# Small and wide matmul rounds grouped, and the 16 small tiles of a round taken image by image

## What is computed

```python
x = x + _L0_conv_ref(_gn(x), w3, b3, w5, b5, wr, br)   # a 3x3 and a 5x5 convolution, 9 shifts of the
                                                       # first, mixed by wr: one 5x5 filter with a border ring
x = x + _L1_conv_ref(_gn(x), filters)                  # all products of two values of the 10 (a one and
                                                       # the 3x3 patch), weighted by a 32x32x10x10 filter
```

## Time and profile before

| | |
|---|---|
| median of 3 runs | 304.58 us (304.39 to 304.66) |
| the profiled execution: own time | 305.6 us |
| its span, first to last instruction | 303.9 us |
| TensorE busy | 276.0 us (91%), 6464 matmul records |
| VectorE busy | 251.5 us (83%) |
| ScalarE busy | 88.1 us (29%) |
| mean granted TensorE clock | 0.979 |

### The profile page before, as it was taken

One profiled execution on the slowest core, in us unless ns is written; L12 is line 12 of the kernel. 1 busy time (PEld: TensorE's weight loads), 2 busy tenths in 40 slices (PEclk: granted clock), 3 DMA queues, 4 the chain that ended last, 5 costly groups with the idle time before them and its releaser, 6 DMA issues.

```text
span 303.9 us, 13566 instructions
## 1 busy us (share of the span) xinstructions
PE 276.0 (91%) x6464; PEld 125.6 (41%) x6464; DVE 251.5 (83%) x216; ACT 88.1 (29%) x135; POOL 33.0 (11%) x82
## 2 busy tenths in 40 slices
PE   0579999899999999999999999999999999999930
PEld 0124443343334434436457455333334446447310
DVE  1899899995999999599999999976999999950330
ACT  5432016949258989529000000004000000000000
POOL 7913970000110000000000000000000000000000
PEclk9999999979999999999999999999999999999985
DMA  6973000000000000000000000085000000000049
GB/s 191 382 193 82 4 3 2 2 5 2 2 2 4 4 2 2 4 2 5 2 2 4 4 2 4 2 172 111 2 2 4 2 2 4 2 4 4 2 86 190
DMA packets 19206, 11.45 MB, mean 38 GB/s; under 512 B 17744, under 2 KB 17872, under 8 KB 19024
## 3 DMA queue, kind: packets, MB, share of 16 engines
q1 hardware_dynamic: 14640, 9.06, 11.7%
q10 hardware_dynamic: 4512, 1.53, 2.2%
HBM read 6.40 MB, written 4.19 MB: 35 GB/s over the span
## 4 chain that ended last, share of the span: by engine, by line
PE 80%; DVE 7%; ACT 3%; issue 3%; DMA 2%; SPq 1%; DVEq 0%
PE acc L1007 63%; PE acc L1050 15%; ACT raw L507 3%; DMA raw<-in_x 2%; DVE stats L741 2%; PE acc L1101 2%; DVE plane L759 1%; DVE raw L801 1%; DVE arena L669 1%; ACT arena L497 1%; DVE scaled L637 0%; DVE norm L756 0%; SPq L314 0%; SPq L321 0%; DVE mean_var L746 0%
## 5 line engine op out<-in xcount | busy, mean ns | idle before, releaser
L1007 PE MATMUL acc<-product,weight 32*32 32x512 f32 (+1 forms) x3040 | 128.6, 605 | 0.0
L1007 PEld LDWEIGHTS acc<-product,weight 32*32 32x32 f32 (+1 forms) x3040 | 61.7, 110 | 63.8 <-issue 51.1
L879 DVE TENSOR_TENSOR product<-plane 128x4096 f32<-128x4096 f32 x19 | 83.3, 4427 | 0.1
L1007 PE MATMUL acc<-raw,weight 32*32 32x512 f32 (+1 forms) x992 | 44.3, 605 | 0.0
L1050 PE MATMUL acc<-product,middle 32*64 32x512 f32 (+1 forms) x576 | 30.6, 621 | 0.0
L1007 PEld LDWEIGHTS acc<-raw,weight 32*32 32x32 f32 (+1 forms) x992 | 20.4, 111 | 20.7 <-issue 16.2
L801 DVE TENSOR_TENSOR raw<-acc,arena 128x512 f32<-128x512 f32 x16 | 9.9, 684 | 18.9 <-issue 18.7
L741 DVE BATCH_NORM_STATS2 stats<-raw 128x6 f32<-128x512 f32 x32 | 19.7, 686 | 3.1 <-DMA raw<-in_x 3.1
L879 DVE TENSOR_TENSOR raw<-plane 128x4096 f32<-128x4096 f32 x5 | 22.2, 4433 | 0.0
L1007 PE MATMUL acc<-product,arena 32*32 32x512 f32 (+1 forms) x448 | 22.0, 606 | 0.0
L507 ACT ACTIVATE raw<-arena 32x512 f32<-32x512 f32 x32 | 21.9, 683 | 0.5
(11 more groups left out here) (121 smaller groups left out, 213.9 us busy)
## 6 DMA issues: line engine op xcount, KB each, us to landing
raw<-in_x SPq DMA_DIRECT2D x8, 512.0 KB, 8.5
out<-raw SPq DMA_DIRECT2D x24, 128.0 KB, 2.9
arena<-in_L_conv_filters SPq DMA_DIRECT2D x4, 400.0 KB, 6.9
out<-raw ACTq DMA_DIRECT2D x8, 128.0 KB, 4.6
arena<-in_L_conv_w ACTq DMA_DIRECT2D x4, 100.0 KB, 4.0
w_in<-in_L_conv_w ACTq DMA_DIRECT2D x2, 36.0 KB, 1.9
w_in<-in_L_conv_w SPq DMA_DIRECT2D x2, 36.0 KB, 2.1
b_in<-in_L_conv_b SPq DMA_DIRECT2D x2, 0.5 KB
```

The lines of the kernel that those rows point to most:

```text
L879: nc.vector.tensor_tensor(both_halves(g, u), plane_halves(g), plane_halves(g, PRODUCTS[k][0] * PITCH + PRODUCTS[k][1]), ALU.mult)\
L1007: return nc.tensor.matmul(acc[32 * s:32 * (s + strips), j, r, :], weights[32 * r:32 * r + 32, t:t + strips, :] .rearrange("p t c -> p (t c ...
```

## The change

Four edits, all to what TensorE issues and in what order; every matmul of before is still there, with the same operands, apart from start and stop flags that follow the order.

1. In `column`, a small round loops over images outside and strips inside (`column0`, the same form in stage 1, keeps its order).
2. The units of stage 2 that were issued as wide, small or small, wide one by one are issued in groups: several units wide, then the same units small.
3. Around the borders of group 1 in stage 1, two rounds of the wide form of "total" stand between the row edges and the column edges, where its small round stood, and the parts after them begin with the small form; in stage 2 the plane's small rounds stand ahead of the row edges, and its wide rounds between the two sets of edges.
4. Products (1,-2) and (2,-1) change places, for VectorE, GpSimd and TensorE alike.

```diff
-PRODUCTS = ((0, 0), (0, 1), (1, 1), (1, -1), (0, 2), (2, 2), (2, -2), (2, 1), (1, 2), (2, -1), (1, -2), (2, 0), (1, 0))
+PRODUCTS = ((0, 0), (0, 1), (1, 1), (1, -1), (0, 2), (2, 2), (2, -2), (2, 1), (1, 2), (1, -2), (2, -1), (2, 0), (1, 0))
 N_PRODUCTS = len(PRODUCTS)
...
-                    for s in range(STRIPS):
-                        for r in range(GROUP):
+                    for r in range(GROUP):
+                        for s in range(STRIPS):
                             d, t = (lo, 0) if s % 2 else (hi + 1, hi - lo)
                             last = tile(r, s, 1, d, t, start, stop)
                 return last
@@ -1041,7 +1041,7 @@
...
             product0(1, "next", 0, True, False, True)
             product0(1, "next", 0, False, False, False)
             edges0(0, ROW_SIDES)
-            product0(1, "total", 0, False, False, False)
+            product0(1, "total", 0, False, False, True, (-1, 0))
             edges0(0, COLUMN_SIDES)
-            product0(1, "total", 0, False, True, True).then_inc(part_done, 1)
+            product0(1, "total", 0, False, False, True, (1, 2))
+            product0(1, "total", 0, False, True, False).then_inc(part_done, 1)
             pe.wait_ge(edges_copied, 2)
-            rest0(1, PAIRS_FIRST)
+            rest0(1, SINGLES_FIRST)
...
                 if g == 0:
                     pe.wait_ge(even_ready, NG)
                     for half in (0, 1):
-                        column(0, plane_pixels(0, half), every_row, sum_taps[0][:, 0:3, :], half == 0, False, PAIRS)
+                        column(0, plane_pixels(0, half), every_row, sum_taps[0][:, 0:3, :], half == 0, False, SINGLES)
                     edges0(1, ROW_SIDES)
                     for half in (0, 1):
-                        column(0, plane_pixels(0, half), every_row, sum_taps[0][:, 0:3, :], False, False, SINGLES)
+                        column(0, plane_pixels(0, half), every_row, sum_taps[0][:, 0:3, :], False, False, PAIRS)
                     edges0(1, COLUMN_SIDES)
                     pe.wait_ge(borders, 5)
-                    mixed_unit(g, 0, "square", SP, stop=True).then_inc(shared_done, 1)
+                    mixed_unit(g, 0, "square", SINGLES)
+                    mixed_unit(g, 0, "square", PAIRS, stop=True).then_inc(shared_done, 1)
                     pe.wait_ge(edges_copied, 2 * NG)
+                    mixed_unit(g, 1, "linear", PAIRS, start=True)
+                    mixed_unit(g, 1, "square", PAIRS)
+                    mixed_unit(g, 1, "linear", SINGLES).then_inc(unit_used, 1)
+                    mixed_unit(g, 1, "square", SINGLES, stop=True).then_inc(unit_used, 1)
+                    pe.wait_ge(shared_kept, 1)
+                    side_unit(g, 0, "linear", SINGLES, start=True)
+                    side_unit(g, 0, "square", SINGLES)
+                    wait_made(g, NEXT)
+                    taps1(g, 0, NEXT, SINGLES)
+                    side_unit(g, 0, "linear", PAIRS)
+                    side_unit(g, 0, "square", PAIRS)
+                    taps1(g, 0, NEXT, PAIRS)
+                    pe.wait_ge(shared_kept, 2)
+                    side_unit(g, 1, "linear", PAIRS, start=True)
+                    side_unit(g, 1, "square", PAIRS)
+                    taps1(g, 1, NEXT, PAIRS)
+                    side_unit(g, 1, "linear", SINGLES).then_inc(unit_used, 1)
+                    side_unit(g, 1, "square", SINGLES).then_inc(unit_used, 1)
+                    taps1(g, 1, NEXT, SINGLES).then_inc(unit_used, 1)
+                    in_pairs = False
                 else:
                     pe.wait_ge(borders, 6)
                     pe.wait_ge(evicted, GROUP)
-                    mixed_unit(g, 0, "linear", PS, start=True)
-                    mixed_unit(g, 0, "square", SP)
+                    mixed_unit(g, 0, "linear", PAIRS, start=True)
+                    mixed_unit(g, 0, "square", PAIRS)
                     pe.wait_ge(stream_made, made(g, "next"))
                     column(0, stream_pixels(g, NEXT, 0), every_row, next_sum, False, False, PAIRS)
+                    mixed_unit(g, 0, "linear", SINGLES)
+                    mixed_unit(g, 0, "square", SINGLES)
                     column(0, stream_pixels(g, NEXT, 0), every_row, next_sum, False, True, SINGLES)\
                         .then_inc(shared_done, 1)
                     pe.wait_ge(evicted, 2 * GROUP)
-                mixed_unit(g, 1, "linear", SP if g else PS, start=True).then_inc(unit_used, 1)
-                mixed_unit(g, 1, "square", PS if g else SP, stop=True).then_inc(unit_used, 1)
...
-                in_pairs = g == 0
+                    mixed_unit(g, 1, "linear", SINGLES, start=True)
+                    mixed_unit(g, 1, "square", SINGLES)
+                    mixed_unit(g, 1, "linear", PAIRS).then_inc(unit_used, 1)
+                    mixed_unit(g, 1, "square", PAIRS, stop=True).then_inc(unit_used, 1)
+                    pe.wait_ge(shared_kept, 3)
+                    side_unit(g, 0, "linear", PAIRS, start=True)
+                    side_unit(g, 0, "square", PAIRS)
+                    side_unit(g, 0, "linear", SINGLES)
+                    side_unit(g, 0, "square", SINGLES)
+                    side_unit(g, 0, "next", SINGLES)
+                    side_unit(g, 0, "next", PAIRS)
+                    pe.wait_ge(shared_kept, 4)
+                    side_unit(g, 1, "linear", PAIRS, start=True)
+                    side_unit(g, 1, "square", PAIRS)
+                    side_unit(g, 1, "next", PAIRS)
+                    side_unit(g, 1, "linear", SINGLES).then_inc(unit_used, 1)
+                    side_unit(g, 1, "square", SINGLES).then_inc(unit_used, 1)
+                    side_unit(g, 1, "next", SINGLES).then_inc(unit_used, 1)
+                    in_pairs = False
```

More of the change, by code:

```diff
@@ L1042, in plane_pixels, with column0 @@
                 return pixels
-            def column0(odd, stack, at, pitch, x0, every, five, start, stop, pairs):
+            def column0(odd, stack, at, pitch, x0, every, five, start, stop, pairs, rows):
                 def tile(r, s, strips, d, t, first_one, last_one):
@@ L1054, in column0 @@
                 if pairs:
-                    for d in range(-1, 3):
+                    for d in rows:
                         for s in (0, 2):
@@ L1064, in column0, with product0 @@
                 return last
-            def product0(g, name, odd, start, stop, pairs):
+            def product0(g, name, odd, start, stop, pairs, rows=range(-1, 3)):
                 if name == "next":
@@ L1070, in product0 @@
                     return column0(odd, plane[g], PLANE_AT - 2 * PITCH, PITCH, 2, 2, weight0[:, PAIR_AT:EDGE_AT, :],
-                                   start, stop, pairs)
+                                   start, stop, pairs, rows)
                 source, x0 = ("step", 1) if name == "step after" else (name, 0)
@@ L1077, in product0 @@
                 pe.wait_ge(middle_ready, g + 1)
-                return column0(odd, *half_at(g, source), x0, 1, five, start, stop, pairs)
+                return column0(odd, *half_at(g, source), x0, 1, five, start, stop, pairs, rows)
             def part(g, names, odd, forms):
@@ L1169, in mixed_unit, with side_unit @@
                     taps = (cross_taps if j else sum_taps)[0][:, 3:6, :]
-                for pairs in forms:
-                    last = column(j, stream_pixels(g, UNIT_OF[name][0], j), every_row, taps,
-                                  start and pairs == forms[0], stop and pairs == forms[-1], pairs)
-                return last
-            def side_unit(g, j, name, forms, start=False):
+                return column(j, stream_pixels(g, UNIT_OF[name][0], j), every_row, taps, start, stop, pairs)
+            def side_unit(g, j, name, pairs, start=False):
                 pe.wait_ge(stream_made, made(g, name + (" right" if j else " left")))
@@ L1181, in side_unit @@
                     a = {"linear": 0, "square": 9}[name] + 6 * j
-                for pairs in forms:
-                    last = column(j, stream_pixels(g, UNIT_OF[name][1], j), every_row, weight1[:, a:a + 3, :],
-                                  start and pairs == forms[0], False, pairs)
-                return last
+                return column(j, stream_pixels(g, UNIT_OF[name][1], j), every_row, weight1[:, a:a + 3, :],
+                              start, False, pairs)
             def taps1(g, j, u, pairs, stop=False):
@@ L1227, in _ @@
                     pe.wait_ge(evicted, 2 * GROUP)
-                mixed_unit(g, 1, "linear", SP if g else PS, start=True).then_inc(unit_used, 1)
-                mixed_unit(g, 1, "square", PS if g else SP, stop=True).then_inc(unit_used, 1)
-                pe.wait_ge(shared_kept, 2 * g + 1)
-                side_unit(g, 0, "linear", SP if g else PS, start=True)
-                side_unit(g, 0, "square", PS if g else SP)
-                if g:
-                    side_unit(g, 0, "next", SP)
-                else:
-                    wait_made(g, NEXT)
```

(13 more changed lines are left out.)

3 lines of the change are left out of this document (1 added, 2 removed).

## The result

| | before | after |
|---|---|---|
| median | 304.66 us, 7 runs (304.39 to 305.73) | 302.79 us, 7 runs (301.44 to 304.24) |
| the profiled execution: own time, span | 305.6, 303.9 us | 304.24, 302.5 us |
| mean granted TensorE clock in it | 0.979 | 0.984 |

The ratio is 0.9925, with a 95% interval from 0.9899 to 0.9952: 0.75% faster. The forecast was 300.6 us, 2.2 too low. All ratios leave out one execution of the kernel before, 406.97 us at a mean granted clock of 0.663.

A forecast was written before the change was run, and what follows sets the result against it. TensorE, busy 91% of the span and holding 80% of the last-ending chain, was taken as the bound. 303.9 - 2.5 - 1.5 = 299.9 us of span, 301.6 own time, median 1.0 lower: 300.6 us; 8-in-10 range 297.2 to 304.6.

The forecast's parts named there:

- Term 1: Borders of stage 1: shorter instruction gap and a clock that stays high start stage 2 at 89.2, gain 2.2 us.
- rival B: Small rounds: image order makes them dearer, 0.10 us per round, 114 rounds, +11.9 us, 312.5 us; chance 0.18.
- C: Small rounds after unit 16: image order makes them cheaper, at 0.05 us each 3.0 us less, 297.6 us; chance 0.14.
- D: Stage 2: gain goes into new waits, a buffer given back later stops VectorE; 303.1 or 304.4 us; chance 0.09.
- Term 2: Start of stage 2 to the cross sum, then to unit 16: the new order makes of 2.2 a gain of 2.5.
- The wait for the left part of the square: First group of stage 2: TensorE wants VectorE's left part of the square 0.9 us too soon.
- Term 3: From unit 16 to the end: wide stretches fall from 12 to 8, 4 x 0.38 = 1.5 us gained.
- Term 4: Small rounds, image by image: number of instructions ahead matters, so 0 per round; bounds -0.235 to +0.41 us.
- A: Border of stage 1: the clock falls anyway, costing 1.7 us of the gain there, 302.3 us; chance 0.17.

The follow-up runs named there:

- second_group: The kernel before with the grouped stretches of the linear, square and next units in group 1 of stage 2 alone, three wide stretches fewer: 303.94 us, ratio 0.997.
- after_again: The changed kernel once more, nothing edited, a second profiled execution: 301.90 us, ratio 0.9917.
- more_switches: The changed kernel with units from 7 on in group 1 always wide then small, two wide and two small stretches more: 303.40 us, ratio 0.9952.
- no_swap: The changed kernel with products (2,-1) and (1,-2) where they were before: 303.69 us, ratio 0.9964.
- joined: The changed kernel with the wide rounds of unit 9 joined to those of units 7 and 8, small rounds after them: 301.61 us, ratio 0.9885.
- twice: The changed kernel with, in group 1, both halves' matmuls in a row for each small-round tile, 8 instructions before the next tile's: 327.36 us, ratio 1.075.
- shift_code: The kernel before with 40 tiny matmuls, 160 instructions, ahead of everything: 305.17 us, ratio 1.0014.
- image_only: The kernel before with image order in the small rounds alone, nothing grouped: 305.21 us, ratio 1.0015.
- strip_order: The changed kernel with the small rounds of stage 2 strip by strip again: 302.62 us, ratio 0.9926.

## Why the prediction was right, and where 2.2 us are missing

The time fell into the range, 297.2 to 304.6, and the gain was 1.9 us by the medians where 4.0 were forecast. More than half of the 4.0 had no base in the kernel. That the time is in the range all the same is luck as far as term 1 goes: the range was wide for the sake of rivals B, C and D.

**Term 1, borders: the step that failed.** Parts of the mechanism were seen: the gap shrank to 0.22 (predicted 0.5) and the clock stayed up. But the 2.2 us that it took as the kernel's loss were those of one execution. Beside the other four with its border, the profiled execution took 34.76 - 32.55 = 2.2 us more for this path, 1.7 for the slow clock and 0.5 for the longer gap. What the new order itself brought was 0.2 us. The slow clock is rare rather than excluded: of 76 executions of the kernel before that were timed beside the experiments, two had a mean clock of 0.979 as in the profile, and took 306.64 and 306.69 us; one of second_group had 0.980 and 304.87 us. In 70 timed executions with the new border none is below 0.982. Where the clock fell in those three no trace shows, and so few do not show that the new order prevents it. The medians hardly feel it.

**The base.** The forecast started the row edges at 56.69, as in the profile. In the thirteen others they start between 56.96 and 59.04, with a mean of 57.89, so the profiled execution was 1.2 us early there, lost 2.2 us on the path, and came out 1.0 above the median. From there to stage 2 I forecast 89.2 - 56.69 = 32.5 us, and measured was 32.3 on the average: the path was right, its start 1.2 early for a typical run. Then the step "the median stands 1.0 below the profiled execution's own time" took off once more what term 1 had taken off already. 1.2 and 1.0, with a few tenths either way from the other terms, are the 2.2 us.

**Term 2: right in sum, but not in its waits.** From stage 2 to its second group the forecast gives 103.9 (the 18.8 us from unit 16 on as before); the four profiles with this order gave 103.58 to 104.13, mean 103.79. L544 stands 18.1 us behind the start of stage 2 (forecast 18.4); that it would start at 107.6 hung on term 1 and the base, and in after_again, without the early gap, it starts at 107.51. The row edges were to take 1.1 us and wait 0.3 for L673. L673 ends at 94.08 in after and the edges start at 94.23, behind their own two rounds; they took 1.57 to 2.16 us, with a gap of their own as shown above. The wait for the left part of the square was 0.3 in place of 0.9 (VectorE idle 1.95 before its L872, which had 0.57), and the six small rounds around it took 7.26 us, about 0.6 more than six took before.

**Term 3: right, a little too large.** Group 1 has four wide stretches fewer, for which 1.5 were forecast; measured 95.61 - 94.33 = 1.28, 0.32 each. Single edits gave 0.29 (more_switches), 0.30 (second_group), 0.47 (no_swap) and 0.60 (joined): the price of a stretch is not the same everywhere, and 0.38 is near the middle of the four. That part of the price lies in how the queue refills at a change of tile form is argued from the loads, not shown.

**Term 4: right.** Nothing per round, as taken; the run twice bears out the reason given. The count of rounds was not right: `column0` keeps its order, so of the 114 small rounds only the 100 of stage 2 changed theirs, and rival B's 0.10 us each would have been 10.0 us (114 would have been 11.4, not 11.9). Nothing in the forecast hangs on it.

**Rivals.** A did not come: in nine profiles with the new border the clock stayed up. B and C are excluded at 0.007 us per round. D's mechanism, a later buffer that stops VectorE, shows as 1.95 us of idle time, but VectorE had them to spare. What happened is close to the number of A, 302.3, for a reason that was not among the rivals: nearly all of the loss to be removed was one execution's.

Added up for typical runs: 0.2 at the border, 0.5 in group 0 (a mean of 104.31 in the five kernels with its old order, 103.79 in the four with the new) and 1.28 in group 1 give 2.0 us; by the medians of the two measurements the change gained 1.9 and 2.8, by their ratios 2.3 and 2.5. The start of the row edges moves from run to run in good part with a packet of instructions. The wide stretch at 25 us took 7.13 us in seven of fourteen profiles and 7.49 to 9.05 in the rest. shift_code apart, whose packets hold other pieces, the packet had landed 0.6 us or more before the stretch began in the seven, and 0.3 us before to 1.5 us after its begin in the rest, and the later it landed, the more the stretch took. The wait for L673 hides a part of that. Why the packet is late in some executions is open; no experiment was made on it.

## What to carry to other kernels

Before a term is built on a stall or a slow clock in one profile, ask whether it is of the kernel or of that execution: compare the mean clock and the own time with the other runs, and if the profiled execution is above the median, take the excess off once, not also as the gain of the edit that removes its cause. Count the changes between tile forms; each pair costs some 0.3 to 0.6 us here, and grouping rounds by form was a gain that nothing took back in group 1, where VectorE is ahead. Where two limits stand close behind each other, as a VectorE result and TensorE's next instructions do at the borders, easing one is worth no more than the distance to the other.

## What the runs showed of the hardware

- With 16 tiles of 32 x 32 in float32, how many instructions of one tile stand in a row is what counts: 4 a tile give 1.09 us a round, 8 a tile 1.73 (20.78 us for 12) to 1.85 (mean of 32), with the same matmuls. Which tile follows which, at 4 a tile, changes 0.007 us at most (image_only, strip_order).
- TensorE's instructions come in pieces of 16 KB, and a run of short matmuls can outrun them. In the column edges of stage 1, 80 records, the gap was 0.9 to 1.5 us in the five profiles with the old border and nothing to 0.5 in the nine with the new one; in before and after it comes behind the 5th record, and it came behind the 53rd when 160 instructions were put ahead (shift_code). It ends 1.3 to 1.5 us after the end of a packet of 16 KB.
- A granted clock of 0.50 came once in fourteen profiles at this place, in before, where TensorE had been busy 1.86 of the 3.41 us ahead; in the other four with the old border it had been busy 2.29 to 2.50 of 3.40 there, and the clock stayed at 1.00. No run tests what decides it.
